# A three-layer graph attention stack: the first chunk of the first layer summed during the count stage

## What is computed

```python
def gat_layer(x, src, dst, W, a_src, a_dst, b, n_nodes):
    h = x @ W
    s = h @ a_src
    d = h @ a_dst
    e = jax.nn.leaky_relu(s[src] + d[dst], NEG_SLOPE)
    m = jax.ops.segment_max(e, dst, num_segments=n_nodes)
    ex = jnp.exp(e - m[dst])
    z = jax.ops.segment_sum(ex, dst, num_segments=n_nodes)
    alpha = ex / z[dst]
    out = jax.ops.segment_sum(alpha[:, None] * h[src], dst, num_segments=n_nodes)
    return out + b
h = jnp.maximum(_layernorm(x, axis=-1), 0.0)
x = x + _L0_gnn_ref(h, edge_index, ...)   # two such layers
h = jnp.maximum(_layernorm(x, axis=-1), 0.0)
x = x + _L1_gnn_ref(h, edge_index, edge_attr_64, ...)   # the third
```

## Time and profile before

| | us |
|---|---|
| median of 3 runs | 714.85 |
| lowest, highest | 714.55, 715.75 |
| the profiled execution | 714.44 |
| its span, first to last instruction | 712.6 |
| DVE busy, PE busy | 674.7, 604.9 |
| ACT busy, POOL busy | 463.8, 368.3 |
| last one-hot ends (from the span's start) | 198.24 |
| first product of the first layer | 202.76 |

### The profile page before, as it was taken

The page is one execution under the profiler, slowest core; times in us unless marked ns, Lnnn a source line. Parts: engine busy times, 40 slices in busy tenths (PEclk is TensorE's granted clock), DMA queues, the critical chain, the costliest instruction groups (busy, mean ns, idle before and its releaser), DMA issues.

```text
span 712.6 us, 13778 instructions
## 1 busy us (share of the span) xinstructions
PE 604.9 (85%) x5576; PEld 588.5 (83%) x5576; DVE 674.7 (95%) x939; ACT 463.8 (65%) x696; POOL 368.3 (52%) x354
## 2 busy tenths in 40 slices
PE   2657677675589899999999979999989889999995
PEld 1557666665589899999998979898979889999995
DVE  3999999999999999999999799999999989999995
ACT  0326666454497557575666768878776698687780
POOL 5581000000045454454675666758588677696883
PEclk9956889677789999999999999999999999999998
DMA  3410000001000000000100100000010010100001
GB/s 76 112 47 1 2 1 1 1 8 3 35 1 20 1 18 1 19 1 1 9 36 2 26 2 18 1 19 1 2 10 36 1 27 1 36 17 22 19 1 41
DMA packets 22325, 12.07 MB, mean 17 GB/s; under 512 B 12393, under 2 KB 20055, under 8 KB 22255
## 3 DMA queue, kind: packets, MB, share of 16 engines
q1 hardware_dynamic: 21455, 9.85, 5.9%
q0 software_dynamic: 800, 1.26, 0.6%
HBM read 9.47 MB, written 1.64 MB: 16 GB/s over the span
## 4 chain that ended last, share of the span: by engine, by line
DVE 56%; PE 30%; issue 9%; POOL 3%; ACT 1%; DMA 1%; DVEq 0%; POOLq 0%
PE ps L1739 23%; DVE scratch L864 22%; DVE ps L980 15%; DVE scratch L1062 9%; DVE ps L982 2%; DVE ps L992 2%; PE ps L1792 2%; PE ps L1695 1%; PE ps L1770 1%; POOL scratch L673 1%; DVE scratch L980 1%; DMA gathered<-in_edges,start_i 1%; DVE bn L814 1%; PE ps L1762 1%; PE ps L1795 0%
## 5 line engine op out<-in xcount | busy, mean ns | idle before, releaser
L1739 PE MATMUL ps<-hB,scratch 125*125 125x129 f32 x3450 | 404.2, 276 | 23.9 <-DVE scratch L1062 20.3
L1739 PEld LDWEIGHTS ps<-hB,scratch 125*125 125x125 f32 x3450 | 390.8, 189 | 32.2 <-DVE scratch L1062 24.5
L673 POOL TENSOR_TENSOR scratch<-scratch,C 125x625 f32<-125x625 f32 x197 | 250.8, 1284 | 178.9 <-ACT scratch L1500 178.9
L980 DVE SCALAR_TENSOR_TENSOR ps<-C,a_unit,ps 125x625 f32<-125x625 fp8e3 x330 | 278.0, 868 | 2.3
L1498 ACT ACTIVATE scratch<-gathered,r_neg 125x625 f32<-125x625 f32 x197 | 159.3, 809 | 43.1 <-PE ps L1739 40.9
L1500 ACT ACTIVATE scratch<-scratch,r_src 125x625 f32<-125x625 f32 x197 | 160.9, 817 | 6.4
L1062 DVE SCALAR_TENSOR_TENSOR scratch<-ps,r_src,C 125x625 f32<-125x625 f32 x178 | 153.5, 862 | 5.7 <-PE ps L1729 5.7
L1695 PE MATMUL ps<-scratch 128*128 128x125 bf16 x1250 | 105.9, 260 | 49.5 <-DVE scratch L864 49.5
L1695 PEld LDWEIGHTS ps<-scratch 128*128 128x128 bf16 x1250 | 99.8, 120 | 55.4 <-DVE scratch L864 54.1
L1363 ACT ACTIVATE C<-ps 125x1500 fp8e3<-125x1500 f32 (+2 forms) x60 | 75.3, 1270 | 73.8 <-PE ps L1695 73.5
L864 DVE TENSOR_TENSOR scratch<-key_lo,ps 128x5376 bf16<-128x5376 bf16 (+3 forms) x31 | 87.8, 2833 | 0.2 <-PE ps L1695 0.2
(11 more groups left out here) (185 smaller groups left out, 419.4 us busy)
## 6 DMA issues: line engine op xcount, KB each, us to landing
gathered<-g_lines SPq DMA_DIRECT2D x15, 305.2 KB
xr<-in_x SPq DMA_DIRECT2D x1, 1562.5 KB
out<-xr SPq DMA_DIRECT2D x4, 312.5 KB
edge_sb<-in_edges SPq DMA_DIRECT2D x1, 805.7 KB
gathered<-ext_lines SPq DMA_DIRECT2D x5, 122.1 KB
w<-in_W SPq DMA_DIRECT2D x2, 128.0 KB
out<-xr SPq DMA_DIRECT2D x1, 187.5 KB
out<-xr SPq DMA_DIRECT2D x1, 125.0 KB
```

The lines of the kernel that those rows point to most:

```text
L673: g.tensor_tensor(slot[s], slot[s], C5[:, q % NC, s, :], ALU.mult).then_inc(pool_done, 1)
L980: v.scalar_tensor_tensor(dest, counts, unit[:, s:s + 1], top, ALU.min, ALU.max).then_inc(S.top_done, 1)
L1739: last = mm(ps[0:P, acc_at(t):acc_at(t) + HW], A[:, P * t:P * (t + 1)], feat, start=opens and t in (0, 3), stop=closes, skip_group_check=True)
```

## The change

Tiles of the count stage have at most 16 windows (eight tiles a chunk, seven of 16 and one of 13; NT = 40), halves have eight windows and lie in other PSUM banks, so that the banks of the sums are free during the stage. The ring moves behind the one-hots. The other chunks' keys are transposed at tiles 5 to 8, the seven feature rounds run at tiles 9 to 15, the extremes at 16, the scalars after tile 18, the exponentials at 19. POOL alone makes the 25 blocks of chunk 0 (`first_maximum`, then the product), scales the features in five operations, and PE sums the blocks behind the counts of tiles 23 to 37. ACT forms the row maxima of chunk 1's blocks 0 to 5 behind tiles 38 and 39. DVE starts the layer with chunk 1; the top steps of chunks 0 to 3 are spread over chunks 1 to 3 (FIRST_TOPS), more blocks of these go to POOL (OWN lists DVE's), and the work after the sums moves to later slots (FIRST_LAYER). Layers two and three stay as they are. The diff, cut to its core:

```diff
     BIG = 1e30
+    LARGEST = 3.4028234663852886e38
     MAGIC = 12582912.0
     assert T * P == N and NW * WQ == N and WG * P == NW and EP * P == E and NS * SAMPLE == EP
     assert EX % U == 0 and WC == P
-    SPLIT = (0, 21, 42, 63, 84, 105, P)
+    SPLIT = (0, 16, 32, 48, 64, 80, 96, 112, P)
     JT = len(SPLIT) - 1
     NT = NC * JT
-    WMAX = 21
+    WMAX = 16
     COLS = 128
...
-        ring = [scratch[0:P, i * CD:(i + 1) * CD] for i in range(RING + 1)]
+        ring = [scratch[0:P, 2 * OH + i * CD:2 * OH + (i + 1) * CD] for i in range(RING)]
...
         G0T, AB0 = 3584, 3584 + 4 * P
-        HALF = [(0, 12, 0), (12, WMAX, 2048)]
+        HALF = [(0, 8, 1024), (8, WMAX, 2048)]
         LAST_AT = 3072
-        IOTA = 1536
+        IOTA = 3072
         iota_ps = ps[:, IOTA:IOTA + COLS * LANES // 2].bitcast(bf16).rearrange("p (c n) -> p c n", c=COLS)
...
         FEATS = tuple((t, min(t + 4, T)) for t in range(0, T, 4))
-        FEAT_AT = (5, 7, 9, 11, 13, 15, 17)
         KEYS_TILE = 4
-        EXT_AT, OVER_AT, EXPS_AT = 20, 23, 24
-        SCALED_AT = 26
-        SCALED = tuple(range(2, 10)) + (0, 1) + tuple(range(10, T))
+        FEAT_AT = tuple(KEYS_TILE + WG + r for r in range(len(FEATS)))
+        EXT_AT = FEAT_AT[-1] + 1
+        OVER_AT = EXT_AT + 2
+        EXPS_AT = OVER_AT + 1
+        EARLY_AT = EXPS_AT + 2
+        LAG = 2
+        EARLY_TO = NT - 2 - LAG
+        EARLY = {t: tuple(range((t - EARLY_AT) * T // (EARLY_TO - EARLY_AT), (t + 1 - EARLY_AT) * T // (EARLY_TO - EARLY_AT)))
+                 for t in range(EARLY_AT, EARLY_TO)}
+        AHEAD_OF_LAYERS = {NT - 2: (0, 1, 2), NT - 1: (3, 4, 5)}
...
                    At(1, (3, 4, 5, 6), 6, (8, 9, 10), None, (14, 17, 20), (None,) * 3, (None,) * 3, None, None))
+        FIRST_LAYER = (None,
+                       At(14, (15, 15, 16, 16), 16, (17, 17, 18), None, (23,), (21, 23, 27), (23, 25, 29), 25, 27),
+                       At(10, (11, 11, 12, 12), 12, (13, 13, 14), None, (20,), (17, 20, 25), (19, 22, 27), 22, 24),
+                       At(4, (5, 5, 6, 6), 6, (7, 7, 8), None, (16,), (13, 16, 22), (15, 18, 24), 19, 21))
...
+        OWN = ((), (15, 17, 19, 21, 23), (1, 4, 6, 8, 10, 12, 14, 16, 18, 20, 22), (1, 4, 7, 10, 13, 16, 18, 20, 22))
+
+        def spread_tops(q, k0, k1, s0, s1):
+            return tuple((s0 + (k - k0) * (s1 - s0) // (k1 - k0), q, k) for k in range(k0, k1))
+
+        AFTER = T
+        FIRST_TOPS = (None,
+                      spread_tops(0, AHEAD, T, 0, 13) + spread_tops(1, 0, 10, 14, 25) + spread_tops(1, 10, 14, AFTER, AFTER),
+                      spread_tops(1, 14, T, 0, 10) + spread_tops(2, 0, 17, 10, 25) + spread_tops(2, 17, 21, AFTER, AFTER),
+                      spread_tops(2, 21, T, 0, 4) + spread_tops(3, 0, T, 4, 24) + spread_tops(4, 0, AHEAD, AFTER, AFTER))
+
         def pool_tiles(q):
+            if q < len(OWN):
+                return tuple(s for s in range(T) if s not in OWN[q])
...
                      for q in range(NC, Q, NC)}
         def post_at(q):
             L = (q - 1) // NC
+            if q < len(FIRST_LAYER):
+                return FIRST_LAYER[q]
             return TURN[L] if turn(q) else BEFORE_LAST[L] if q % NC == NC - 1 and L < 2 else USUAL[L]
...
         LAST_ODD = max(k for k in range(T) if in_odd(k))
+
+        def tops_before_rows(q):
+            if q in (2, 3):
+                c, k = min((c, k) for at_, c, k in FIRST_TOPS[q - 1] if at_ == AFTER)
+                return c * (T + 1) + k
+            return q * (T + 1) if q > 1 else 0
...
                 sp.wait_ge(lines_stored, 16 * LINES[L, 0 if L == 0 or c < EARLY_TILES // CT else EARLY_TILES])
-                if q > 1:
-                    sp.wait_ge(over_done, pool_no(q - 1, 0))
+                if q == 2:
+                    sp.wait_ge(first_max, T)
+                elif q > 2:
...
+            def first_maximum(s):
+                if s == 0:
+                    pool.wait_ge(ga_loaded, 16)
+                if s >= RING and s != T - 1:
+                    pool.wait_ge(F.pe_done, slot_free(s))
+                g.tensor_scalar(slot[s], ga[0], LARGEST, r_src[0][:, s:s + 1], ALU.min, ALU.max).then_inc(first_max, 1)
+
             def block_product(q, s):
-                pool.wait_ge(rowmax_ok, pool_no(q, s) + 1)
+                if q == 0:
+                    first_maximum(s)
+                    pool.wait_ge(first_max, s + 1)
+                else:
+                    pool.wait_ge(rowmax_ok, act_no(q, s) + 1)
                 g.tensor_tensor(slot[s], slot[s], C5[:, q % NC, s, :], ALU.mult).then_inc(pool_done, 1)
...
                 t1 = t0 + CT
-                pool.wait_ge(exps_ready, EXPS[L, 0 if t0 < EARLY_TILES else t0])
-                pool.wait_ge(F.pe_done, (L * NC - 1) * T + t1)
+                pool.wait_ge(exps_ready, EXPS[L, 0 if L == 0 or t0 < EARLY_TILES else t0])
+                if L:
+                    pool.wait_ge(F.pe_done, (L * NC - 1) * T + t1)
+                else:
+                    pool.wait_ge(keys_sb, 2 * WG)
+                    pool.wait_ge(h_ones, 1)
...
                             scale_tiles(L, LATE)
-                    if q < NC and s in B2_AT:
+                    if q == 0 and s % CT == 0:
+                        scale_tiles(0, s)
+                    if 0 < q < NC and s in B2_AT:
                         second_bias(q * CT + B2_AT.index(s))
                     if q == Q - 1 and s == 22:
                         last_bias()
                     if s in POOL_OF[q]:
                         block_product(q, s)
+                if q == 0:
+                    for t in range(CT):
+                        second_bias(t)
 
             for q in range(Q):
...
-                dve.wait_ge(F.rows_ready, q + 1)
+                dve.wait_ge(F.rows_ready, q)
                 v.scalar_tensor_tensor(slot[s].rearrange("p (t n) -> p t n", n=P), tiles(ROWU), r_src[L % 2][:, s:s + 1],
...
+                for at_, c, k in FIRST_TOPS[q]:
+                    if at_ == s:
+                        next_top(c, k)
+                        if k == T - 1:
+                            join_tops(F, c)
 
             def chunk(q):
...
                     elif s == 0:
-                        dve.wait_ge(F.rows_ready, q + 1)
-                    for k in range(AHEAD, T):
-                        if top_at(q, k) == s:
-                            next_top(q, k)
-                    if s == join_at(q):
-                        join_tops(F, q)
+                        dve.wait_ge(F.rows_ready, q)
+                    if q < len(FIRST_TOPS):
+                        first_tops(q, s)
+                    else:
+                        for k in range(AHEAD, T):
+                            if top_at(q, k) == s:
+                                next_top(q, k)
+                        if s == join_at(q):
+                            join_tops(F, q)
                     if q:
                         at_ = post_at(q)
...
                         set_mode(L)
-                if q < Q - 1:
+                if q < len(FIRST_TOPS):
+                    first_tops(q, AFTER)
+                elif q < Q - 1:
...
                 next_top(0, k)
-            for q in range(Q):
+            for q in range(1, Q):
                 chunk(q)
             last_result()
...
                 a_.activation(g_row[L % 2][:, t0:t1], b_cut[L % 2][:, t0:t1], ACT.Exp,
                               bias=sigma[L % 2][:, :]).then_inc(g_done, 1)
 
-            def scale_features(s):
-                a_.activation(hB3[:, s, :], hA[:, s, :], ACT.Copy, scale=e_src[0][:, s:s + 1]).then_inc(h_scaled, 1)
-
-            for t in range(NT):
-                c, j = t // JT, t % JT
-                if c < NC - 1 and j == KEYS_TILE:
-                    copy_keys(c + 1)
-                if t + 1 in FEAT_AT:
-                    normalise_first(FEAT_AT.index(t + 1))
-                if t in FEAT_AT:
-                    features_out(FEAT_AT.index(t))
-                if t == EXPS_AT:
-                    act.wait_ge(sig_ready, 1)
-                    exps_src(0, 0, T)
-                    exps_dst(0, 0, T)
-                if t >= SCALED_AT:
-                    if t == SCALED_AT:
-                        act.wait_ge(exps_ready, 1)
-                        act.wait_ge(h_ones, 1)
-                    for s in SCALED[2 * (t - SCALED_AT):2 * (t - SCALED_AT) + 2]:
-                        scale_features(s)
-                counts_out(t, 0)
-                if t in FEAT_AT:
-                    attention_out(FEAT_AT.index(t))
-                counts_out(t, 1)
+            def first_negative_r():
+                act.wait_ge(exps_ready, 1)
+                a_.activation(r_neg[0][:, :], r_src[0][:, :], ACT.Copy, scale=-1.0).then_inc(rneg_ready, 1)
...
                 act.wait_ge(over_done, k + 1)
                 a_.activation(A, A, ACT.Identity, bias=r_src[L % 2][:, s:s + 1]).then_inc(rowmax_ok, 1)
 
+            def count_stage():
```

(74 more changed lines are left out.)

45 lines of the change are left out of this document (20 added, 25 removed).

## The result

The changed kernel took 706.25 us (median of four runs, 705.08 to 707.76) against 715.11 (714.55 to 715.75): a ratio of 0.988, 95% interval 0.986 to 0.990, so 8.9 us or 1.2% faster. The forecast was 703.0 in a range of 693 to 713. The profiled execution took 705.08 (span 703.2), where the sum had said 702.6, and 9.4 less than the profiled one of before. One later execution was slow from end to end, the first of the variant e3_rows (1212.9 us, 449 ns a matmul of the sums instead of 277), and no comparison here uses it.

The account below looks back on a forecast made before the run. VectorE's one-hots bound the count stage, VectorE and TensorE together the layer. 714.4 - 24.0 - 3.7 + 1.3 + 0.7 + 5.5 + 1.0 + 1.4 + 5.0 + 1.0 = 702.6 us, as median 703.0, range 693 to 713.

Parts of the forecast that it names:

- One-hots, +1.3: Count stage: smaller one-hot tiles make five chunks 1.3 us longer in all.
- x, +0.7: Before the node statistics: x lands at 36.3 us, tiles 0 to 3 end at 35.7, costing 0.7 us.
- Feature ring, +5.5: Tiles 9 to 15: rounds through ACT and PE take 5.45 us against a 4.35 pitch; +5.5, ends 3 and 9.
- give back 2: Feature rounds: the short tile 15 and the slow clock return 2 us of the cost.
- Late count stage, +1.0: PE's blocks beside the counts fill 3.9 of 4.35 us a tile; +1 us, ends 0 and 8.
- rival C: Late count stage: the clock falls in every third tile, +11 us, giving 713; chance 0.14.
- POOL's blocks, hidden with 5.5 us of cover: Count stage: 25 blocks at 2.25 us end 5.5 us before PE's need, so POOL costs nothing.
- rival B: POOL's maximum runs at the one-operation rate, 1.8 us, and PE waits in tiles 23 to 37: 722; chance 0.12.
- Rival D: VectorE and POOL exclude one another, each POOL instruction waiting half a one-hot: 757 us; chance 0.02.
- Waits for row transposes ahead of chunks 2 to 4, -3.7: First layer: DVE's waits of 1.22 us at three chunk starts go, saving 3.7 us.
- The reduction of chunk 1, +5.0: Chunk 1: DVE reaches the reduction before PE's top transpose and stalls 5.0 us, ends 2 and 7.
- Rival A: The stalls of the feature rounds and chunk 1's start don't come: 690.6 us; chance 0.14.

Follow-up runs that it names:

- e3_rows: All six row maxima of chunk 1 placed behind tile 39's copy-outs, against the changed kernel: 707.36 us, ratio 0.988.
- e10_inside: On e8_spread, GpSimd waits for VectorE's coverage-test product ahead of its two additions, not behind them: 694.22 us, ratio 0.971.
- e0_after: The changed kernel run again, nothing altered, beside three variants: 708.58 us, ratio 0.990.
- e4_oneop: POOL's maximum written with one operation instead of two, against the changed kernel: 724.06 us, ratio 1.016.
- e2_sums: Move of chunk 0's sums placed ahead of row maxima 3 to 5 in ScalarE's queue, against the changed kernel: 705.01 us, ratio 0.986.
- e5_chain: Chunk 1's reduction of the tops and what follows it up to three slots later, against the changed kernel: 704.99 us, ratio 0.986.
- e9_spread_only: Row maxima 0 to 2 one by one behind tiles 36, 37 and 38, against the changed kernel: 702.43 us, ratio 0.985.
- e1_ring: Next round's normalisations placed behind the feature copy-out in ScalarE's queue, against the changed kernel: 701.65 us, ratio 0.982.
- e7_all: The edits of e1_ring, e2_sums and e5_chain together on the changed kernel: 697.66 us, ratio 0.975.
- e6_ring_sums: The edits of e1_ring and e2_sums together on the changed kernel: 699.39 us, ratio 0.978.
- e8_spread: On e7_all, row maxima 0 to 2 one by one behind tiles 36, 37 and 38: 695.34 us, ratio 0.973.

## Why the prediction was right, step by step

**To the last one-hot, +8.5 predicted, +6.7 measured.**
- One-hots, +1.3. In e10_inside, with every other cost of the stage gone but 0.2 us for x, they end at 199.60, 1.4 later than before, so 1.2 without x. Tiles start their one-hots 2.20 and 2.15 us apart (from 120.03 to 124.38 for a tile). Right, though 7 x 4.35 + 3.55 is 34.00 and not 33.97, which gives +1.5.
- x, +0.7: the statistics waited 0.17 us, in the variants up to 0.93.
- Feature ring, +5.5: 3.9 in the profiled execution. Its links were right in kind: a round took 5.1 here, 5.45 were summed. The size isn't a constant, though. It was 3.5 to 3.9 at a clock of 0.88, 4.9 and 6.9 at 0.79 and 0.80, 11.2 and 11.1 at 0.66, so the upper end of 9 was too low. The prediction's "give back 2" has the right sign (5.5 comes out only as 5.5 - 2 of slack + 2), but it was too small: where the clock stayed at the lower level a round took 6.64 us, 2.3 over the pitch instead of the 1.1 that was summed. That 3.9 came out near 5.5 is partly the luck of an execution at 0.88. The 2.3 us between the medians of e0_after and the first one would fit the same cause, which the profiled executions show and the others cannot.
- Late count stage, +1.0: nothing. The 32 counts took 2.07 us and two blocks 2.42, at a granted clock of 1.00; rival C did not come. The busier TensorE was at 2.4 GHz throughout, where the same stage of before showed 0.74.
- Not in the sum at all: the product of the coverage test, 2.33 us instead of 1.19, +1.1 (e10_inside). The four tiles ahead of the node statistics now take 17.4 us instead of 22.6, so it ran at 42.6 and met GpSimd's additions; before it ran at 47.6, with GpSimd idle.

1.2 + 0.2 + 3.9 + 1.1 = 6.4 of the 6.7.

**POOL's blocks, hidden with 5.5 us of cover.** Right: 7.6 us. The start was 18.0 us after tile 18's end (114.38; 17.4 predicted, where the terms given, 4 + 8.5 + 3.9, make 16.4), TensorE asked 84.3 after it (84), the maximum 0.79 (0.8), the block 2.15 (2.25). The choice between the two tensor_scalar rows was the step that carried the sign: e4_oneop shows the other one, 1.85 us a maximum and 724.06 us, where rival B had 722 and its break-even at 1.5 us. Rival D is out too: one-hots take 2.29 and 2.23 us beside POOL's products and without them, and VectorE is busy 74.00 of 74.00.

**Chunks 1 to 3, -20.3 predicted, -17.3 measured.**
- Products, -24.0: VectorE's work fell by 23.0.
- Waits for row transposes ahead of chunks 2 to 4, -3.7: all gone, as forecast. But one of 0.8 us at the start of chunk 5 before became one of 2.0 (362.81), and that is most of the +1.3 behind chunk 4, which the sum did not have.
- Rows ahead of chunk 1, +1.4: 1.83. TensorE's first block at 11.1 us after the last one-hot: 10.7. The reduction of chunk 1, +5.0: 5.21. The chain of ScalarE's queue was worked out right (TensorE's start within 0.4 us), and e2_sums, e5_chain and e9_spread_only each shortened it as that chain says: by an earlier start of TensorE, by a later asking, and by a shorter queue ahead of both.
- "Later chunks have the transpose at slots 10 and 4, where PE is no longer late": wrong. The reductions of chunks 2 and 3 waited 0.89 and 0.80 us. This step failed, by 1.7 us.
- Other small waits, +1.0: idle time that belongs to no wait above was 0.9 in the stretch before (4.5 less 3.6) and 1.7 after (10.4 less 1.8 and 6.9), so +0.8.

The three parts are off by -1.8, +3.0 and +1.3: 2.5 us on the profiled execution, 3.3 on the median. The mechanism was right in all large terms; the misses are of sizes and partly cancel. Rival A (no stalls, 690.6) did not come by itself, but the edits of e10_inside take the kernel most of the way there, to 694.22. The prediction's price of rival C is one off: 11 over its 703.0 is 714.

Of the clock and the ring, the traces settle two things. The lower level lengthens the ring: a round takes 6.64 us in e2_sums, at 0.50 throughout, and 5.10 in the changed kernel at 76 to 81 us, mostly at full clock. And VectorE's waits on the ring do not start the fall: read in stretches of 2 us from 60 on, the clock first comes down to 0.50 to 0.57 between 66 and 76 us in every variant of the table, with the ring (e0_after at 68, first wait of VectorE at 76.0; the changed kernel at 74, first wait at 84.7) and without it (e1_ring at 68, e7_all at 74), and the kernel before, which waited 0.2 us, shows 0.83 in 60 to 101. Left open is whether the ring then keeps the clock down: e1_ring, e6_ring_sums, e7_all, e8_spread and e10_inside, without it, show 0.92 to 0.95 there, and those with it 0.66 to 0.88, but no run holds one of the two fixed.
